# Second attention: the first pass's tiles issued whole and early in a step, and the output copy moved from VectorE to ScalarE

## The chip, the cores and the metric

The kernel runs on one core of a Trainium2 chip. The metric is device time in microseconds (us) for one execution. A core has a matrix engine (TensorE, in profiles PE, with its weight loads shown apart as PEld), a vector engine (VectorE, DVE), a scalar engine (ScalarE, ACT), GpSimd (POOL) and SyncE (SP), which issues the DMA transfers. Each engine works through its own instructions in order. They wait for each other through semaphores. Products of TensorE land in PSUM, from where DVE and ACT read them; POOL reads and writes SBUF alone.

## The reference

Two transformer layers follow one another on x of shape (4, 1024, 512), with 16 heads of 32 columns each. The first has a distance bias in its attention; the second has quantised linear layers and plain attention. The change touches only the second attention:

```
attn = softmax(einsum('bhqd,bhkd->bhqk', q, k) * hd ** (-0.5))   # per head: 1024 x 1024 scores
o    = einsum('bhqk,bhkd->bhqd', attn, v)                        # per head: 1024 x 32
```

There are 4 x 16 = 64 heads.

## The kernel before

The program is six stages with a barrier of all engines between them: the first layer's projections, attention and MLP, then the second's (`build_program`). `stage_attention1` is the second attention. q and k are held as high and low parts, so that one product over 96 rows (hi.hi, hi.lo, lo.hi) gives the scores at nearly full precision. Every head is computed in two passes:

- **First pass** (`score`, L707 to L714). A tile u has 128 queries as its partitions and 1024 keys as columns, in PSUM `s`, made by two products of 512 columns. DVE reduces each tile to the minimum of its rows (`minimum`, L799; q carries a factor of -1, so the minimum of a row is its softmax maximum). There are 8 tiles in a head, and `s` is a ring of 2 tiles: the first product of tile u+2 waits until DVE has reduced tile u. In tables of this document such a product is an `s` product.
- **Between the passes** POOL splits the 8 minima of each partition in two parts (`mm`), TensorE turns them to rows (`turn_minima`, L748), DVE copies these out (`mr`, L810), and SyncE puts them as rows 97 and 98 beside q.
- **Second pass** (`score_turned`, L716 to L723). The same scores again, turned: 128 keys as partitions and 512 queries as columns, with the minima taken in by the added rows. A tile is one product into PSUM `st`, a ring of 3 buffers of 512 columns. ACT takes the exponential of each into `PT` (`exponential`, L784). These are `st` products below. The rows that are turned, the minima's and the output's, take a buffer of the same ring.
- **Sums.** `times_v` multiplies `PT` by v into the left half of PSUM `po` (L733). POOL adds pairs of `PT` tiles into `two` (L866), and `total` multiplies those by ones into the right half of `po` (L741). `take_output` copies `po` to `ov` (L812 to L817), TensorE turns `ov` (`turn_output`, L754), and DVE divides (`output`, L819 to L831).

The work goes in steps w of 4 tiles (half a head), pipelined by hand: step w holds the first pass of tiles 4w to 4w+3, the second pass of tiles 4(w-4) and on, the products with v of step w-5, and in every second step a totals part or an output part. Steps in which the minima and the totals of a head stand are called even here, and those in which `ov` is copied and turned odd. A head takes one even and one odd step. There are 128 steps of first pass; in steps 4 to 127, 124 in number, both passes run side by side.

Nothing but the order in the code of each engine and the waits decides when something runs. Within a step the order on TensorE before is `st s st s` for each of the first three tiles and `st s s st` for the fourth: 8 `st` and 8 `s` products. The copy of `po` stands on DVE behind the first minimum of an odd step.

Of the kernel before, what the change touches and what calls it, by code (L numbers as in the profile page):

```python
# [6 lines left out]
ACT, ALU, AX = mybir.ActivationFunctionType, mybir.AluOpType, mybir.AxisListType  # L7

P = 128
B, L, D, H, F = 4, 1024, 512, 16, 2048  # L10
HD = D // H
T = B * L
DC, FC, LT = D // P, F // P, L // P
BLK = 512
# [382 lines left out]
N_HEADS = B * H  # L397
# [239 lines left out]
def stage_attention1(K):  # L637
# [4 lines left out]
    nc, a, pe, dve, act, pool, sp = K.nc, K.a, K.pe, K.dve, K.act, K.pool, K.sp  # L642
    ROWS = 3 * HD
    NW, TAIL = N_TILES // 4, 7
    with Stage(K, "T1") as S:
# [7 lines left out]
        ov = [S.sb(f"ov1{i}", [P, 2 * QW]) for i in range(2)]  # L653
        rec = [S.sb(f"rec1{i}", [P, 2, 4]) for i in range(2)]
        og = S.stores("og1", 2, [P, LT, GRP * HD])
        ps_r = S.ps_ring("s1", 2, [P, L])
        pst_r = S.ps_ring("st1", 3, [P, BLK])
        po = S.ps("po1", [P, 2 * QW])
        s_neg, s_score, s_min, s_mm, s_mt, s_mr, s_st, s_exp, s_two, s_pv, s_sum = (S.sem() for _ in range(11))
        s_row = [S.sem() for _ in range(2)]  # L660
        s_ov, s_turn, s_rec, s_out = (S.sem() for _ in range(4))
# [43 lines left out]
                store_group(g)  # L705
            og.done(sp)

        def score(u, g):
            n, t = divmod(u, LT)
            p, j = divmod(n, PAIR)  # L710
            qs, ks = qs_l.ready(pe, p), ks_l.ready(pe, p)
            ps = ps_r.take(pe, u, (s_min, u + 1)) if g == 0 else ps_r.at[u]
            nc.tensor.matmul(ps[:, g * BLK:(g + 1) * BLK], qs[0:ROWS, j, t * P:(t + 1) * P],  # L713
                             ks[0:ROWS, j, g * BLK:(g + 1) * BLK], start=True, stop=True).then_inc(*s_score.up())  # L714

        def score_turned(u, g):  # L716
            n, kb = divmod(u, LT)
            p, j = divmod(n, PAIR)
            pe.wait_ge(s_row[n % 2], 32 * (n // 2 + 1))
            pe.wait_ge(s_neg, 1)  # L720
            ps = pst_r.take(pe, ("st", u, g), (s_exp, 2 * u + g + 1))
            nc.tensor.matmul(ps[:], ks_l.at[p][0][0:ROWS + 2, j, kb * P:(kb + 1) * P], qs_l.at[p][0][0:ROWS + 2, j, g * BLK:(g + 1) * BLK],  # L722
                             start=True, stop=True).then_inc(*s_st.up())  # L723

        def times_v(u):
            n, kb = divmod(u, LT)
            p, j = divmod(n, PAIR)
            v = v_l.ready(pe, p)
            pe.wait_ge(s_exp, 2 * u + 2)
            if kb == 0:  # L730
                pe.wait_ge(s_ov, n)
            for g in range(4):
                op = nc.tensor.matmul(po[g * HD:(g + 1) * HD, 0:QW], v[:, kb, j * HD:(j + 1) * HD],  # L733
                                      pT[n % 2][:, kb, g * QW:(g + 1) * QW], start=kb == 0, stop=kb == LT - 1)
            op.then_inc(*s_pv.up())

        def total(m):
            n, k = divmod(m, LT // 2)
            pe.wait_ge(s_two, m + 1)
            for g in range(4):  # L740
                op = nc.tensor.matmul(po[g * HD:(g + 1) * HD, QW:2 * QW], K.ones[:, 0:HD], two[m % 6][:, g * QW:(g + 1) * QW],  # L741
                                      start=k == 0, stop=k == LT // 2 - 1)
            op.then_inc(*s_sum.up())

        def turn_minima(n):
            ps = pst_r.take(pe, ("min", n), (s_mr, n + 1))
            pe.wait_ge(s_mm, n + 1)
            nc.tensor.transpose(ps[0:2 * LT, 0:P], mm[n % 2][:].bitcast(F32).rearrange("p a t -> p (a t)"), K.ident[:]).then_inc(*s_mt.up())  # L748

        def turn_output(n):  # L750
            ps = pst_r.take(pe, ("out", n), (s_out, n + 1))
            pe.wait_ge(s_ov, n + 1)
            for i in range(2 * QW // P):
                op = nc.tensor.transpose(ps[:, i * P:(i + 1) * P], ov[n % 2][:, i * P:(i + 1) * P], K.ident[:])  # L754
            op.then_inc(*s_turn.up())

        def tensor_program():
            for w in range(NW + TAIL):
                for i in range(4):
                    if 0 <= w - 4 < NW:  # L760
                        score_turned(4 * (w - 4) + i, 0)
                    if w < NW:
                        score(4 * w + i, 0)
                    if w < NW and i == 3:
                        score(4 * w + i, 1)
                    if 0 <= w - 4 < NW:
                        score_turned(4 * (w - 4) + i, 1)
                    if w < NW and i < 3:
                        score(4 * w + i, 1)
                n, odd = divmod(w - 2, 2)  # L770
                if not odd and 0 <= n < N_HEADS:
                    turn_minima(n)
                n, odd = divmod(w - 7, 2)
                if not odd and 0 <= n < N_HEADS:
                    turn_output(n)
                if 0 <= w - 5 < NW:
                    for i in range(4):
                        times_v(4 * (w - 5) + i)
                n, odd = divmod(w - 6, 2)
                if not odd and 0 <= n < N_HEADS:  # L780
                    for i in range(LT // 2):
                        total(n * LT // 2 + i)

        def exponential(u, g):  # L784
            n, kb = divmod(u, LT)
            if n >= 2:
                act.wait_ge(s_pv, (n - 2) * LT + kb + 1)
                act.wait_ge(s_two, (n - 2) * LT // 2 + kb // 2 + 1)
            act.wait_ge(s_st, 2 * u + g + 1)
            nc.scalar.activation(pT[n % 2][:, kb, g * BLK:(g + 1) * BLK], pst_r.at["st", u, g][:], ACT.Exp, scale=-1.0).then_inc(*s_exp.up())  # L790

        def scalar_program():
            for w in range(NW + TAIL):
                if 0 <= w - 4 < NW:
                    for i in range(4):
                        exponential(4 * (w - 4) + i, 0)
                        exponential(4 * (w - 4) + i, 1)

        def minimum(u):  # L799
            n, t = divmod(u, LT)  # L800
            if t == 0 and n >= 2:
                dve.wait_ge(s_mm, n - 1)
            dve.wait_ge(s_score, 2 * (u + 1))
            nc.vector.tensor_reduce(mn[n % 2][:, t:t + 1], ps_r.at[u][:], AX.X, ALU.min).then_inc(*s_min.up())  # L804

        def take_minima(n):
            if n >= 2:
                dve.wait_ge(s_row[n % 2], 32 * (n // 2))
            dve.wait_ge(s_mt, n + 1)
            nc.vector.tensor_copy(mr[n % 2][:], pst_r.at["min", n][0:2 * LT, 0:P]).then_inc(*s_mr.up())  # L810

        def take_output(n):  # L812
            dve.wait_ge(s_pv, (n + 1) * LT)
            dve.wait_ge(s_sum, (n + 1) * LT // 2)
            if n >= 2:
                dve.wait_ge(s_turn, n - 1)
            nc.vector.tensor_copy(ov[n % 2][:], po[:]).then_inc(*s_ov.up())  # L817

        def output(n):  # L819
            h = n % H  # L820
# [15 lines left out]
        def vector_program():  # L836
            for w in range(NW + TAIL):
                if w < NW:
                    minimum(4 * w)
                n, odd = divmod(w - 7, 2)  # L840
                if not odd and 0 <= n < N_HEADS:
                    take_output(n)
                if w < NW:
                    for i in range(1, 4):
                        minimum(4 * w + i)
                n, odd = divmod(w - 2, 2)
                if not odd and 0 <= n < N_HEADS:
                    take_minima(n)
                n, odd = divmod(w - 7, 2)
                if not odd and 0 <= n < N_HEADS:  # L850
                    output(n)
# [28 lines left out]

        sync_program()
        tensor_program()
        vector_program()
        scalar_program()
        gpsimd_program()

# [1296 lines left out]
```

## Time and profile before

| | before |
|---|---|
| median of 3 runs (lowest to highest) | 3962.01 us (3960.73 to 3963.63) |
| the profiled execution: its own time | 3961.7 us |
| its span in the trace | 3959.9 us |
| second attention | from 2554 to about 3585 us of the span |
| busy over the whole span: PE, PEld, DVE, ACT, POOL | 93%, 62%, 63%, 58%, 42% |

Times in rows are microseconds from the start of the span, unless a column says ns. The duration of a matmul row is the time in the array with its pipeline, so two rows overlap; the distance between the starts of two products says how fast TensorE goes. A product that had to wait is shown from where it could start.

### The profile page before, as it was taken

The page shows a single profiled execution, that of the slowest core. Times are in us where ns is not written, and L with a number is a line of the kernel's source. Part 1 is how long each engine was busy: PE and PEld are TensorE (multiplying, and loading weights), DVE is VectorE, ACT ScalarE, POOL GpSimd, SP SyncE. Part 2 cuts the span into 40 slices and gives each one's busy share as a digit, 9 for nine tenths or more (in the row PEclk, how much of TensorE's full clock was granted, in tenths as well). Part 3 has the DMA queues.
Part 4 walks back from the last instruction along what each step waited for, and adds up shares of the span by engine and source line. Part 5 has one row for each costly group of instructions (what it writes and reads, how often), then busy time and mean ns, then how long its engine had stood idle before and what let it go on. Part 6 is the DMA issues. An engine that isn't in the chain of part 4 may idle for free. (4 is left out here: it accounts for less than half of the span.)

```text
span 3959.9 us, 68031 instructions
## 1 busy us (share of the span) xinstructions
PE 3671.7 (93%) x25924; PEld 2449.5 (62%) x25924; DVE 2510.9 (63%) x4095; ACT 2285.4 (58%) x3963; POOL 1672.8 (42%) x1931
## 2 busy tenths in 40 slices
PE   8997999999999987899999959799999999995999
PEld 7885666666666665778888845355555555552555
DVE  4335888888888867344431128676666666664987
ACT  2226888888888856222222218555555555554988
POOL 0004555555555557000000017466666666664554
PEclk9998999999999999999999979899999999997999
DMA  5445233333333179334431127823333333313221
GB/s 188 184 165 150 60 65 63 68 63 68 62 68 63 31 229 303 128 131 146 157 122 67 59 85 263 277 50 77 69 63 68 63 68 70 77 33 131 78 78 51
DMA packets 309604, 419.91 MB, mean 106 GB/s; under 512 B 90472, under 2 KB 167788, under 8 KB 309274
## 3 DMA queue, kind: packets, MB, share of 16 engines
q1 hardware_dynamic: 309280, 415.56, 37.4%
q8 instruction: 207, 3.39, 0.4%
q14 instruction: 117, 0.96, 0.1%
HBM read 257.34 MB, written 157.32 MB: 105 GB/s over the span
## 5 line engine op out<-in xcount | busy, mean ns | idle before, releaser
L790 ACT ACTIVATE PT<-st 128x512 f32<-128x512 f32 x1024 | 547.2, 604 | 482.4 <-PE st L722 473.6
L804 DVE TENSOR_REDUCE mn<-s 128x1 f32<-128x1024 f32 x512 | 598.6, 1219 | 336.8 <-PE s L713 236.5
L628 POOL TENSOR_SCALAR biastile<-dist,ascale 128x1024 f32<-128x1024 f32 x512 | 576.2, 1125 | 497.1 <-DVE mn L583 482.8
L866 POOL TENSOR_TENSOR two<-PT 128x1024 f32<-128x1024 f32 x256 | 608.6, 2378 | 364.9 <-ACT PT L790 364.8
L583 DVE CUSTOM_DVE_ANT_0 Sn<-sp,biastile 128x1024 f32<-128x1024 f32 x512 | 624.5, 1220 | 145.0 <-PE sp L489 113.5
L555 ACT ACTIVATE Sn<-Sn,mn 128x1024 f32<-128x1024 f32 x512 | 587.4, 1147 | 19.0 <-DVE mn L583 19.0
L521 PEld LDWEIGHTS pt<-ident,Sn 128*128 128x128 f32 x4096 | 440.5, 141 | 210.5 <-issue 206.7
L521 PE MATMUL pt<-ident,Sn 128*128 128x128 f32 x4096 | 561.6, 280 | 0.6 <-DVE PT L547 0.2
L713 PE MATMUL s<-KS,QS 96*128 96x512 f32 x1024 | 418.5, 432 | 79.1 <-DVE mn L804 46.5
L545 ACT ACTIVATE PT<-pt 128x512 f32<-128x512 f32 x640 | 369.4, 598 | 117.8 <-PE pt L521 117.8
L722 PE MATMUL st<-QS,KS 98*128 98x512 f32 x1024 | 421.6, 413 | 1.5 <-ACT PT L790 1.2
L1328 ACT ACTIVATE gf<-pf,b1T 128x512 f32<-128x512 f32 x128 | 88.3, 690 | 537.8 <-PE pf L1273 533.0
L489 PE MATMUL sp<-KS,QS 97*128 97x512 f32 x1024 | 366.8, 440 | 21.1 <-DMA KS<-cpad 18.7
L1734 POOL MEMSET rcD<- 128x128 bf16 x2 | 0.3, 206 | 775.0 <-POOLq L131 775.0
L510 PE MATMUL po<-PT,Vp 128*32 128x256 f32 x4096 | 325.7, 391 | 0.0
L1419 DVE TENSOR_TENSOR gl<-gf,gh 128x512 fp32r<-128x512 f32 x128 | 88.7, 693 | 372.8 <-ACT gh L1332 370.2
L713 PEld LDWEIGHTS s<-KS,QS 96*128 96x128 f32 x1024 | 186.7, 193 | 215.4 <-DVE mn L804 167.6
L547 DVE COPY PT<-pt 128x512 f32<-128x512 f32 x384 | 265.6, 692 | 59.4 <-PE pt L521 59.3
L722 PEld LDWEIGHTS st<-QS,KS 98*128 98x128 f32 x1024 | 194.4, 190 | 94.6 <-issue 51.9
L733 PE MATMUL po<-PT,Vp 128*32 128x256 f32 x4096 | 247.3, 382 | 0.0
L1284 PE MATMUL pacc<-w2h,gh 128*128 128x512 f32 x512 | 202.1, 395 | 0.6 <-DVE gl L1419 0.6
L1284 PE MATMUL pacc<-w2l,gh 128*128 128x512 f32 x512 | 202.3, 395 | 0.0
(257 smaller groups left out, 6099.8 us busy)
## 6 DMA issues: line engine op xcount, KB each, us to landing
QS<-s_qhi SPq DMA_DIRECT2D x128, 256.0 KB, 5.1
KS<-s_khi SPq DMA_DIRECT2D x128, 256.0 KB, 7.1
KS<-s_klo SPq DMA_DIRECT2D x64, 256.0 KB, 6.1
QS<-s_qlo SPq DMA_DIRECT2D x64, 256.0 KB, 6.9
Vp<-s_v SPq DMA_DIRECT2D x64, 256.0 KB, 7.7
s_o<-og SPq DMA_DIRECT2D x32, 512.0 KB, 4.1
xA<-in_x SPq DMA_DIRECT2D x8, 1024.0 KB, 5.8
s_qhi<-qstage SPq DMA_DIRECT2D x32, 256.0 KB, 2.0
```

What stands on the lines that cost most here:

```text
L489: op = nc.tensor.matmul(ps[:, g * BLK:(g + 1) * BLK], qs[0:rows_s, j, t * P:(t + 1) * P], ks[0:rows_s, j, g * BLK:(g + 1) * BLK], start=Tr ...
L521: op = nc.tensor.transpose(ps[:, i, :], sn[:, (g * HALF + i) * P:(g * HALF + i + 1) * P], K.ident[:])
L545: nc.scalar.activation(dst, src, ACT.Copy).then_inc(*s_cp_act.up())
L555: nc.scalar.activation(sn[:], sn[:], ACT.Exp, scale=-1.0, bias=mn[n % 3][:, t:t + 1], accum_out=sums[n % 5][:, t:t + 1]).then_inc(*s_exp.up())
L583: nc.vector.tensor_tensor_reduce(sn[:], sp_r.at[s][:], bt[s % 2][:], 1.0, 3.4e38, ALU.add, ALU.min, m).then_inc(*s_min.up())
L628: nc.gpsimd.tensor_scalar(bt[s % 2][:], dist[:, t, :], K.ascale[:, n % H:n % H + 1], 1.0, ALU.mult, ALU.mult).then_inc(*s_bias.up())
L713: nc.tensor.matmul(ps[:, g * BLK:(g + 1) * BLK], qs[0:ROWS, j, t * P:(t + 1) * P], ks[0:ROWS, j, g * BLK:(g + 1) * BLK], start=True, stop= ...
L722: nc.tensor.matmul(ps[:], ks_l.at[p][0][0:ROWS + 2, j, kb * P:(kb + 1) * P], qs_l.at[p][0][0:ROWS + 2, j, g * BLK:(g + 1) * BLK], start=Tr ...
L790: nc.scalar.activation(pT[n % 2][:, kb, g * BLK:(g + 1) * BLK], pst_r.at["st", u, g][:], ACT.Exp, scale=-1.0).then_inc(*s_exp.up())
L804: nc.vector.tensor_reduce(mn[n % 2][:, t:t + 1], ps_r.at[u][:], AX.X, ALU.min).then_inc(*s_min.up())
L866: nc.gpsimd.tensor_tensor(two[m % 6][:], pT[n % 2][:, 2 * k, :], pT[n % 2][:, 2 * k + 1, :], ALU.add).then_inc(*s_two.up())
L1284: op = nc.tensor.matmul(pacc[t][:], x[:, t * P:(t + 1) * P], w[:, f, :], start=f == 0 and n == 0, stop=f == FC - 1 and n == 2)
```

## The change

In TensorE's program the two products of a first-pass tile now stand together (`score(u)` without a half), and only the second of them raises the semaphore. A step's pattern is a list of pairs, (how many `st` products, then whether a whole `s` tile): `(1, 1), (1, 1), (3, 1), (2, 1), (1, 0)`. The copy of `po` to `ov` leaves DVE and is made by ACT with the function Copy, ahead of the exponentials of its step. DVE's four minima then stand in a row. The semaphores that the copy waits for and raises stay the same.

```diff
-        def score(u, g):
+        def score(u):
             n, t = divmod(u, LT)
             p, j = divmod(n, PAIR)
             qs, ks = qs_l.ready(pe, p), ks_l.ready(pe, p)
-            ps = ps_r.take(pe, u, (s_min, u + 1)) if g == 0 else ps_r.at[u]
-            nc.tensor.matmul(ps[:, g * BLK:(g + 1) * BLK], qs[0:ROWS, j, t * P:(t + 1) * P],
-                             ks[0:ROWS, j, g * BLK:(g + 1) * BLK], start=True, stop=True).then_inc(*s_score.up())
+            ps = ps_r.take(pe, u, (s_min, u + 1))
+            for g in range(L // BLK):
+                op = nc.tensor.matmul(ps[:, g * BLK:(g + 1) * BLK], qs[0:ROWS, j, t * P:(t + 1) * P],
+                                      ks[0:ROWS, j, g * BLK:(g + 1) * BLK], start=True, stop=True)
+            op.then_inc(*s_score.up())
 
         def tensor_program():
+            n_turned = n_first = 0
             for w in range(NW + TAIL):
-                for i in range(4):
+                for turned, first in ((1, 1), (1, 1), (3, 1), (2, 1), (1, 0)):
                     if 0 <= w - 4 < NW:
-                        score_turned(4 * (w - 4) + i, 0)
-                    if w < NW:
-                        score(4 * w + i, 0)
-                    if w < NW and i == 3:
-                        score(4 * w + i, 1)
-                    if 0 <= w - 4 < NW:
-                        score_turned(4 * (w - 4) + i, 1)
-                    if w < NW and i < 3:
-                        score(4 * w + i, 1)
+                        for _ in range(turned):
+                            score_turned(*divmod(8 * (w - 4) + n_turned, 2))
+                            n_turned = (n_turned + 1) % 8
+                    if w < NW and first:
+                        score(4 * w + n_first)
+                        n_first = (n_first + 1) % 4
 
+        def take_output(n):
+            act.wait_ge(s_pv, (n + 1) * LT)
+            act.wait_ge(s_sum, (n + 1) * LT // 2)
+            if n >= 2:
+                act.wait_ge(s_turn, n - 1)
+            nc.scalar.activation(ov[n % 2][:], po[:], ACT.Copy).then_inc(*s_ov.up())
+
         def scalar_program():
             for w in range(NW + TAIL):
+                n, odd = divmod(w - 7, 2)
+                if not odd and 0 <= n < N_HEADS:
+                    take_output(n)
                 if 0 <= w - 4 < NW:
...
-            dve.wait_ge(s_score, 2 * (u + 1))
+            dve.wait_ge(s_score, u + 1)
...
-        def take_output(n):
-            dve.wait_ge(s_pv, (n + 1) * LT)
-            dve.wait_ge(s_sum, (n + 1) * LT // 2)
-            if n >= 2:
-                dve.wait_ge(s_turn, n - 1)
-            nc.vector.tensor_copy(ov[n % 2][:], po[:]).then_inc(*s_ov.up())
...
                 if w < NW:
                     minimum(4 * w)
-                n, odd = divmod(w - 7, 2)
-                if not odd and 0 <= n < N_HEADS:
-                    take_output(n)
+                    minimum(4 * w + 1)
                 if w < NW:
-                    for i in range(1, 4):
-                        minimum(4 * w + i)
+                    minimum(4 * w + 2)
+                    minimum(4 * w + 3)
```

On TensorE, the first twelve products of an odd step before (`st` second pass, `s` first pass):

```order
L722 MATMUL st<-QS,KS 128x512
L713 MATMUL s<-KS,QS 128x512
L722 MATMUL st<-QS,KS 128x512
L713 MATMUL s<-KS,QS 128x512
L722 MATMUL st<-QS,KS 128x512
L713 MATMUL s<-KS,QS 128x512
L722 MATMUL st<-QS,KS 128x512
L713 MATMUL s<-KS,QS 128x512
L722 MATMUL st<-QS,KS 128x512
L713 MATMUL s<-KS,QS 128x512
L722 MATMUL st<-QS,KS 128x512
L713 MATMUL s<-KS,QS 128x512
```

And now, on TensorE, the whole of an odd step's 16 products and the four that turn `ov` (L714, L724 and L756 are the lines L713, L722 and L754 of before):

```order
L724 MATMUL st<-QS,KS 128x512
L714 MATMUL s<-KS,QS 128x512 x2
L724 MATMUL st<-QS,KS 128x512
L714 MATMUL s<-KS,QS 128x512 x2
L724 MATMUL st<-QS,KS 128x512 x3
L714 MATMUL s<-KS,QS 128x512 x2
L724 MATMUL st<-QS,KS 128x512 x2
L714 MATMUL s<-KS,QS 128x512 x2
L724 MATMUL st<-QS,KS 128x512
L756 MATMUL st<-ident,ov 128x128 x4
```

The first tile was complete with the fourth product and is now with the third; the second tile with the eighth and now the sixth. The third tile still begins with the tenth product, the fourth began with the fourteenth and now does too.

On DVE, an odd step and the even one behind it, before (`mn` minima, `ov` the output's copy, `rec` and `og` the division, `mr` the turned minima):

```order
L804 TENSOR_REDUCE mn<-s 128x1
L817 COPY ov<-po 128x512
L804 TENSOR_REDUCE mn<-s 128x1 x3
L827 RECIPROCAL rec<-st 128x8
L831 TENSOR_TENSOR og<-st,rec 128x4x32 x2
L804 TENSOR_REDUCE mn<-s 128x1 x4
L810 COPY mr<-st 16x128
```

And now the same two steps on DVE:

```order
L814 TENSOR_REDUCE mn<-s 128x1 x4
L830 RECIPROCAL rec<-st 128x8
L834 TENSOR_TENSOR og<-st,rec 128x4x32 x2
L814 TENSOR_REDUCE mn<-s 128x1 x4
L820 COPY mr<-st 16x128
```

The copy between the first and the second minimum is gone from here. On ACT it stands once in 16 exponentials now (an odd step and the even one behind it):

```order
L797 ACTIVATE ov<-po 128x512
L790 ACTIVATE PT<-st 128x512 x16
L797 ACTIVATE ov<-po 128x512
L790 ACTIVATE PT<-st 128x512 x16
```

Before, ACT had nothing but exponentials in this stage.

## Rows read from the trace of the kernel before

**Rows 1.** Stretches: us, busy and count per engine, granted clock, DMA share, GB/s
```profile
400.00:600.00 200.00, 200.00 (x1750) 126.11 (x1749) 167.30 (x301) 177.94 (x324) 108.04 (x96) 1.00 0.31 64
3100.00:3300.00 200.00, 188.78 (x1704) 115.16 (x1706) 135.17 (x165) 108.08 (x202) 125.00 (x76) 1.00 0.31 65
```
**Rows 2.** Waits from 2700 to 3500: total us, times, longest us
```profile
ACT PT L790 <- PE st L722: 360.4, 252, 3.6
...
DVE mn L804 <- PE s L713: 174.1, 51, 3.4
PEld s L713 <- DVE mn L804: 128.9, 202, 1.0
```
**Rows 3.** Timeline of PE, an odd step: start, us, engine, line, tiles
```profile
3009.68 0.50 PE L722 MATMUL st<-QS,KS 98*128 98x512 f32 x1
...
3010.50 0.40 PE L713 MATMUL s<-KS,QS 96*128 96x512 f32 x1
...
3011.67 0.40 PE L722 MATMUL st<-QS,KS 98*128 98x512 f32 x1
...
3012.21 0.50 PE L713 MATMUL s<-KS,QS 96*128 96x512 f32 x1
...
3013.02 0.40 PE L722 MATMUL st<-QS,KS 98*128 98x512 f32 x1
...
3013.94 0.73 PE L713 MATMUL s<-KS,QS 96*128 96x512 f32 x2 [0.53 <-DVE mn L804]
...
3014.51 0.40 PE L722 MATMUL st<-QS,KS 98*128 98x512 f32 x1
```
**Rows 4.** Timeline of PE, the even step ahead of it
```profile
3001.37 0.50 PE L722 MATMUL st<-QS,KS 98*128 98x512 f32 x1
...
3003.36 0.40 PE L722 MATMUL st<-QS,KS 98*128 98x512 f32 x1
...
3003.97 0.50 PE L713 MATMUL s<-KS,QS 96*128 96x512 f32 x1 [0.21 <-DVE mn L804]
...
3004.79 0.40 PE L722 MATMUL st<-QS,KS 98*128 98x512 f32 x1
...
3005.10 0.72 PE L713 MATMUL s<-KS,QS 96*128 96x512 f32 x2
3005.66 0.39 PE L722 MATMUL st<-QS,KS 98*128 98x512 f32 x1
...
3007.84 1.91 PE L741 MATMUL po<-two,ones 128*32 128x256 f32 x32
```
**Rows 5.** Timeline of DVE in the same two steps
```profile
3002.69 4.65 DVE L804 TENSOR_REDUCE mn<-s 128x1 f32<-128x1024 f32 x4 [1.68 <-POOL mm L859]
...
3010.93 1.23 DVE L804 TENSOR_REDUCE mn<-s 128x1 f32<-128x1024 f32 x1 [3.41 <-PE s L713]
...
3012.08 0.68 DVE L817 COPY ov<-po 128x512 f32<-128x512 f32 x1
...
3012.68 3.48 DVE L804 TENSOR_REDUCE mn<-s 128x1 f32<-128x1024 f32 x3
```
**Rows 6.** Timeline of ACT, the odd step; ACT and PE behind the last first-pass tile
```profile
3010.30 3.81 ACT L790 ACTIVATE PT<-st 128x512 f32<-128x512 f32 x7 [3.62 <-PE st L722]
...
3014.94 0.60 ACT L790 ACTIVATE PT<-st 128x512 f32<-128x512 f32 x1 [0.83 <-PE st L722]
...
3561.33 4.03 ACT L790 ACTIVATE PT<-st 128x512 f32<-128x512 f32 x8 [3.49 <-PE st L722]
...
3561.98 2.46 PE L722 MATMUL st<-QS,KS 98*128 98x512 f32 x5 [0.31 <-ACT PT L790]
```
**Rows 7.** Groups from 2700 to 3500: busy us, mean ns, idle before, releaser
```profile
L866 POOL TENSOR_TENSOR two<-PT 128x1024 f32<-128x1024 f32 x203 | 482.7, 2378 | 292.7 <-ACT PT L790 292.7
...
L817 DVE COPY ov<-po 128x512 f32<-128x512 f32 x50 | 34.0, 681 | 0.0
```
**Rows 8.** Groups of ACT from 400 to 1400, in the first attention
```profile
L545 ACT ACTIVATE PT<-pt 128x512 f32<-128x512 f32 x600 | 346.1, 597 | 112.0 <-PE pt L521 112.0
```

## The prediction

> **What bounds the stage.** I read four views in this order. First the stretches: in the middle of the second attention TensorE is busy 188.8 of 200 us at a granted clock of 1.00, DVE 135, POOL 125 and ACT 108 [rows 1]. TensorE is the engine to watch, but not all of its time is work. Then the waits: DVE and ACT wait for TensorE (174 and 360 us in 800), and these waits are the slack of engines that aren't the bound. TensorE in turn waits for something else: its weight load for an `s` product waits 128.9 us for a minimum of DVE, 202 times, which is four times in each of 50.7 heads [rows 2] (203 additions of POOL at four to a head give the same count, and 800 / 50.7 = 15.8 us for a head [rows 7]). Third, the timeline of one odd and one even step, to see which of these waits lengthen the step [rows 3, 4]. Fourth, DVE and ACT in the same steps [rows 5, 6].
>
> I count times in a step from its first `st` product. Without a stall the fourth product stands at 0.82 (3010.50 - 3009.68) and the ninth at 1.99 (3011.67): the first distance is 0.35 and every later one 0.235. So the 16th would stand at 0.35 + 14 x 0.235 = 3.64. It stands at 4.83 in the odd step (3014.51) and at 4.29 in the even one (3005.66 - 3001.37). The stalls cost 1.19 and 0.65 us, 1.84 us for a head.
>
> Each has one form. A product's weights load one slot ahead of it, so a product released late, at r, pays twice: it starts at r, and the next comes 0.35 and not 0.235 later. With L the start of the product ahead of it, its normal slot is L + 0.235, and the delay is r - L - 0.12. The four stalls by that: third tile odd 3012.21 - 3011.67 - 0.12 = 0.42, fourth tile odd 3013.94 - 3013.02 - 0.12 = 0.80, third tile even 3003.97 - 3003.36 - 0.12 = 0.49, fourth tile even 3005.10 - 3004.79 - 0.12 = 0.19 [rows 3, 4]. Their sum is 1.90, against 1.84 read from the starts; the form holds to a few hundredths.
>
> What releases them: in the odd step DVE's first minimum runs 3010.93 to 3012.16, and the third tile starts at 3012.21, 0.05 later. Then comes the copy, so the second minimum starts only at 3012.68, ends 3013.90, and the fourth tile starts at 3013.94 [rows 5]. The copy takes 0.60 of DVE's time there (3012.08 to 3012.68). The even step has no copy and a smaller second stall.
>
> **The change, part by part.**
> The paired tile. The first tile is complete with the third product, at 0.35 + 0.235 = 0.585, and its end is 0.40 behind that, at 0.985. Before it was the fourth (0.82, end 1.22). DVE began 0.03 after that end in the odd step (3010.93 against 3010.90) and 0.10 after in the even one (3002.69, step start 3001.37, so 1.32 against 1.22) [rows 3 to 5]. The first minimum now begins at 1.01 (odd) or 1.08 (even), 0.24 earlier, and frees its buffer at 1.01 + 1.22 + 0.05 = 2.28 or 2.35. The third tile's first product is still the tenth, L = 1.99: delay 0.17 or 0.24, in place of 0.42 and 0.49.
> The second minimum. DVE does a chain of four in 4.65, so 1.14 apart [rows 5]; the second tile is long complete. It frees its buffer at 3.42 (odd) or 3.49 (even). The fourth tile's first product is the fourteenth; the thirteenth then stands at L = 1.99 + 0.235 + 0.17 + 3 x 0.235 = 3.10, or 3.17. Delay 3.42 - 3.10 - 0.12 = 0.20 in both, in place of 0.80 and 0.19. Here the copy's 0.60 goes.
> Three `st` products in a row. `st` has three buffers. ACT starts the first exponential at 0.62 (3010.30), later ones 0.43 after their product (3014.94 against 3014.51), and no closer than 0.49 ((4.03 - 0.60) / 7 in the chain of eight), and a buffer is free 0.05 behind its end (3561.33 + 0.60, product at 3561.98) [rows 3, 6]. The eight `st` products now stand at 0, 0.82, 1.53, 1.76, 1.99, 2.86, 3.10 and 4.01; exponentials start at 0.62, 1.25, 1.96, 2.45, 2.94, 3.43. The seventh product needs the fourth exponential: 2.45 + 0.65 = 3.10, against L = 2.86, a delay of 0.12 by the form; but the fourth tile behind it waits for 3.42 anyway, which swallows it. The eighth needs the fifth, 3.59, and is at 4.01. The turned rows need the sixth, 4.08, against L = 4.01: nothing. No term.
> The copy on ACT. DVE needs 681 ns, ACT 597 for the same shape out of PSUM in the first attention [rows 7, 8]. It stands ahead of an odd step's exponentials and waits for the totals, whose last product ends at 3007.84 + 1.91 = 3009.75, 0.07 into the step [rows 4]. It starts at about 0.15, and at ACT's spacing of 0.49 the first exponential follows at 0.64 to 0.75 in place of 0.62. The second waits for its product until 1.25 either way. The cover is ACT's own wait for TensorE (360 us in 800, [rows 2]). Cost: zero. Its upper bound comes below as a rival. A gain can't come of it on ACT.
> What the copy meets: `po` is free earlier than at 3012.76, and the products with v that need it come after the 16th product. `ov` is needed for turning just there too. No term.
> One semaphore fewer per tile, the same number of products, loads and DMAs: no term. SyncE gets the turned minima as before, behind DVE's fourth minimum, at 1.08 + 4.65 = 5.7 into an even step, and the rows are wanted a step and a half later.
> POOL: four additions of 2.38 and two small operations make some 9.9 us in a head [rows 7], and a head will take 14.7.
>
> Here a rule speaks against the change. The rows say that ACT copies the shape in 0.60 us where DVE takes 0.68 [rows 7, 8]. The Trainium skill, "ScalarE: Activation LUTs", Rules for kernel authors, sends simple elementwise work to VectorE, which per element is up to about three times faster (it has bf16 in mind). By that, as an estimate, the copy would take ACT 3 x 0.68 = 2.04 us, the odd step would lose all it gains, and the time would stay near 3962. The trace prices the very shape and type, so the sum goes by it.
>
> **The sum.** The odd step's 16th product moves from 4.83 to 3.64 + 0.37 = 4.01, 0.82 earlier. The even step's moves from 4.29 to 3.64 + 0.44 = 4.08, 0.21 earlier. What follows the 16th product (turned rows, products with v, totals) waits for nothing that the change delays. 1.03 us for a head, in 124 / 2 = 62 heads' worth of steps in which both passes run: 64 us. In the four first steps only `s` products run, in the last only `st` ones, in the order of before. The other stages are untouched. From the profiled execution's own 3961.7 that gives 3898; the runs' median is 3962.0, 0.3 above, within their spread of 2.9.
>
> **Bounds.** If no stall were left at all, 1.84 x 62 = 114 us go: 3848. If half of the left-over 0.81 us goes too, 3873. On the other side, if ACT doesn't overlap two exponentials when three products come close together, they stand 0.60 apart: 1.96, 2.56, 3.16, 3.76, 4.36. The seventh product is then at 3.21, which the fourth tile's wait nearly swallows, but the turned rows (which need the sixth exponential's buffer) are released at 3.76 + 0.65 = 4.41 against L = 4.01, and pay 4.41 - 4.01 - 0.12 = 0.28 in every step. The gain falls to (1.03 - 0.56) x 62 = 29 us: 3933. The row nearest to the case is the chain of eight at 0.49, so I take that.
>
> **Rivals.**
> (A) The `st` ring becomes the bound, as just worked out: 3933. For it: three `st` products stand together, and ACT has the copy too. Against it: the chain of eight at 0.49 with the same ring [rows 6].
> (B) The stalls stay and only move: DVE starts its minimum earlier but the `s` products stall just as long, because what counts is DVE's spacing; then only the copy's 0.60 in the odd step goes, 0.60 x 62 = 37 us: 3925. Against it: the first minimum starts on the end of a tile, both before and now, and DVE has been idle for 3.41 us there [rows 5].
> (C) Slower: the copy blocks ACT. If it starts at d into the odd step, the first exponential starts at d + 0.49 and its buffer is free at d + 1.14, the next at d + 1.63; the fourth and fifth `st` products wait for these, and from the fifth on the rest takes some 1.8 us, so the 16th product stands at about d + 3.4. Before it was at 4.83. With the even step's 0.21 won, the head is slower from d = 1.6 on. At d = 2 the odd step loses 0.6, a head 0.4, and the time is 3962 + 24 = 3986. For it: ACT was free of any wait on `po`, and everything of the step is queued behind the copy. Against it: the totals end 0.07 into the step, and DVE started within 0.03 to 0.10 of the product it waited for.
> (D) The clock: TensorE's denser work brings a lower granted clock. It would take about 0.93 in the stage to eat 64 us. Against it: in the first attention TensorE is busy 200.00 of 200 us at 1.00 [rows 1]. If the clock fell by half of that, 3930.
> (E) The change does nothing to the time, because TensorE waits elsewhere: 3962. Against it: DVE and ACT both wait for TensorE.
>
> **Numbers.** 3898 has a chance of 0.74, with its own range 3880 to 3912; A and B together 0.13, D's mild form 0.03, C 0.04, E 0.03, and more gained than 3880 says 0.03. Range for 8 in 10: 3878 to 3925. Two executions of this kernel can be told apart from about 0.2%, 8 us. Faster by more: 0.93; within: 0.03; slower: 0.04.
>
> **What would show it.** In the changed kernel's timeline: a head every 14.7 us; the 16th product 4.0 to 4.1 into a step, and both steps alike; the first minimum at 1.0 to 1.1; third tile at 2.3, fourth at 3.4 to 3.5; DVE's four minima in one chain of 4.65 in both steps; the copy on ACT at about 0.15 with 0.60, and the second exponential at 1.25. The wait of `s` weight loads for DVE falls from 0.64 us each to some 0.3. I'd be wrong if the seventh `st` product or the turned rows wait for ACT (A), if the tenth product is as late as before (B), or if the first exponential of an odd step is later than about 1.1 (C).

## The result, and the profile after

| | before | changed |
|---|---|---|
| median | 3962.82 us of 4 (3960.73 to 3964.3) | 3899.4 us of 4 (3897.8 to 3901.37) |
| ratio to before, 95% interval | | 0.9841 (0.9824 to 0.9858) |
| profiled execution, its own time and span | 3961.7, 3959.9 us | 3899.86, 3898.0 us |
| last division of the second attention starts at | 3585.64 us | 3521.60 us |

The kernel is 63 us faster; the interval makes that 56 to 70 us. The forecast was 3898 with a range of 3878 to 3925.

The stretch view, in the middle of the second attention (us, busy and count of PE, PEld, DVE, ACT, POOL, granted clock, DMA share, GB/s), answers to [rows 1]:

```profile
3100.00:3300.00 200.00, 200.00 (x1791) 123.24 (x1789) 137.66 (x166) 124.33 (x234) 132.86 (x83) 1.00 0.36 74
```

TensorE now shows 200.00 us busy in 200, at the same clock. That looks like the end of all waiting. It isn't: a matmul row of 0.40 us overlaps the next, 0.235 behind it, and such an overlap hides a stall of up to 0.16 us. The weight-load column, 123 of 200 us, still has room. The waits of 2700 to 3500, which answer to [rows 2], show what is left:

```profile
DVE mn L814 <- PE s L714: 249.6, 107, 3.2
ACT ov L797 <- PE po L743: 171.9, 54, 3.2
...
PEld st L724 <- ACT PT L790: 48.4, 224, 0.8
PEld s L714 <- DVE mn L814: 46.5, 214, 0.3
```

The weight loads of `s` products wait 46.5 us in place of 128.9, 0.22 each in place of 0.64. And a row is new: the `st` loads wait 48.4 us for ACT's exponentials, 224 times. DVE and ACT now each hold a weight load of TensorE for a short time, four times in a head.

The timeline of PE in one even step (from 3002.31) and one odd step (from 3010.41), against [rows 3, 4]. An x2 row is two products. The second starts 0.235 behind the first, or 0.34 where the first was held:

```profile
3002.31 0.50 PE L724 MATMUL st<-QS,KS 98*128 98x512 f32 x1
...
3004.67 0.73 PE L714 MATMUL s<-KS,QS 96*128 96x512 f32 x2
3005.24 0.64 PE L724 MATMUL st<-QS,KS 98*128 98x512 f32 x2
3005.80 0.73 PE L714 MATMUL s<-KS,QS 96*128 96x512 f32 x2
3006.37 0.40 PE L724 MATMUL st<-QS,KS 98*128 98x512 f32 x1
...
3010.41 0.50 PE L724 MATMUL st<-QS,KS 98*128 98x512 f32 x1
...
3012.69 0.73 PE L714 MATMUL s<-KS,QS 96*128 96x512 f32 x2
3013.25 0.73 PE L724 MATMUL st<-QS,KS 98*128 98x512 f32 x2
3013.82 0.73 PE L714 MATMUL s<-KS,QS 96*128 96x512 f32 x2
3014.39 0.40 PE L724 MATMUL st<-QS,KS 98*128 98x512 f32 x1
```

DVE and ACT in the same steps, against [rows 5, 6]:

```profile
3003.39 4.62 DVE L814 TENSOR_REDUCE mn<-s 128x1 f32<-128x1024 f32 x4 [1.43 <-PE s L714]
...
3010.59 0.60 ACT L797 ACTIVATE ov<-po 128x512 f32<-128x512 f32 x1 [3.18 <-PE po L743]
...
3011.09 4.33 ACT L790 ACTIVATE PT<-st 128x512 f32<-128x512 f32 x8
...
3011.41 4.61 DVE L814 TENSOR_REDUCE mn<-s 128x1 f32<-128x1024 f32 x4 [3.22 <-PE s L714]
```

Read against the start of their steps:

| from the first product of the step | before | forecast | changed |
|---|---|---|---|
| first minimum, odd / even | 1.25 / 1.32 | 1.01 / 1.08 | 1.00 / 1.08 |
| third tile, odd / even | 2.53 / 2.60 | 2.28 / 2.35 | 2.28 / 2.36 |
| fourth tile, odd / even | 4.26 / 3.73 | 3.42 / 3.49 | 3.41 / 3.49 |
| 16th product, odd / even | 4.83 / 4.29 | 4.01 / 4.08 | 3.98 / 4.06 |
| copy on ACT, first exponential, odd | - / 0.62 | 0.15 / 0.64 to 0.75 | 0.18 / 0.68 |

### The profile page after: what moved, and what is told of

Its sections match the earlier page's. It is cut to its first block and busy times, and to the rows that moved or that the text cites. A ratio compares the mean times of both kernels' runs of the same rounds, so it can differ in the third digit from the quotient of the medians.

```text
span 3898.0 us, 67727 instructions
## 1 busy us (share of the span) xinstructions
PE 3656.5 (94%) x25868; PEld 2448.2 (63%) x25924; DVE 2469.4 (63%) x4031; ACT 2316.0 (59%) x4027; POOL 1663.2 (43%) x1931
## 5 line engine op out<-in xcount | busy, mean ns | idle before, releaser
L714 PE MATMUL s<-KS,QS 96*128 96x512 f32 x1024 | 356.8, 431 | 25.0 <-DMA KS<-s_khi 23.6
L724 PE MATMUL st<-QS,KS 98*128 98x512 f32 x1024 | 369.5, 421 | 1.3 <-ACT PT L790 1.3
L724 PEld LDWEIGHTS st<-QS,KS 98*128 98x128 f32 x1024 | 192.8, 189 | 139.0 <-ACT PT L790 59.4
L714 PEld LDWEIGHTS s<-KS,QS 96*128 96x128 f32 x1024 | 177.1, 194 | 106.1 <-DVE mn L814 64.3
```

The costliest lines, as they stand in the source:

```text
L714: op = nc.tensor.matmul(ps[:, g * BLK:(g + 1) * BLK], qs[0:ROWS, j, t * P:(t + 1) * P], ks[0:ROWS, j, g * BLK:(g + 1) * BLK], start=True, ...
```

## The experiments

All changes are to `stage_attention1`. The median of before in these sessions was 3962.6 to 3964.9 us. In the code, `...` marks lines left out, and what stands behind `#` is not in the kernels.

**The copy on ACT alone.** TensorE's order stays as before. Against the kernel before, only `take_output` moves, from DVE's program to ACT's:

```diff
+        def take_output(n):
...
+            nc.scalar.activation(ov[n % 2][:], po[:], ACT.Copy).then_inc(*s_ov.up())
+
         def scalar_program():
             for w in range(NW + TAIL):
+                n, odd = divmod(w - 7, 2)
+                if not odd and 0 <= n < N_HEADS:
+                    take_output(n)
...
-            nc.vector.tensor_copy(ov[n % 2][:], po[:]).then_inc(*s_ov.up())
```

> The order on TensorE as before, only the output's copy moved to ACT. My theory (the stalls are r - L - 0.12 behind DVE's minima): in the odd step the second minimum ends at 1.25 + 1.14 + 1.22 = 3.61, the fourth tile is released at 3.66 against L = 3.34, a delay of 0.20 in place of 0.80: 0.60 x 62 = 37 us gained, 3925. The even step stays at 4.29 for its 16th product. Rival (the copy gains nothing by itself, the early tile does all): 3962. Rival (the copy on ACT delays the first exponentials): above 3962.

Measured: 3926.9 us, ratio 0.9914 (0.9898 to 0.9931), where 3925 was expected. In its timeline the odd step, which starts at 3008.33, has one chain of four minima and the fourth tile 3.66 behind the start, where it was 4.26:

```profile
3009.58 4.64 DVE L814 TENSOR_REDUCE mn<-s 128x1 f32<-128x1024 f32 x4 [3.42 <-PE s L713]
...
3010.86 0.50 PE L713 MATMUL s<-KS,QS 96*128 96x512 f32 x1
...
3011.99 0.72 PE L713 MATMUL s<-KS,QS 96*128 96x512 f32 x2
```

The third tile has not moved (3010.86 - 3008.33 = 2.53). So this half of the change works on the fourth tile of odd steps alone, and is worth 0.60 us a head.

**The order alone.** The changed kernel with `take_output` back on DVE, behind the first minimum:

```diff
                 if w < NW:
                     minimum(4 * w)
+                n, odd = divmod(w - 7, 2)
+                if not odd and 0 <= n < N_HEADS:
+                    take_output(n)                 # on DVE; gone from ACT
+                if w < NW:
                     minimum(4 * w + 1)
```

> TensorE's new order, the copy on DVE behind the first minimum as before. Theory: the first minimum is 0.24 earlier, the third tile's delay falls to 0.17 (odd) and 0.24 (even); the fourth tile in the odd step still waits for copy plus second minimum, 3.42 + 0.60 = 4.02 against L = 3.10, 0.80. Odd 16th product at 3.64 + 0.97 = 4.61 (before 4.83), even at 4.08 (before 4.29): 0.43 x 62 = 27 us, 3935. Rival (the order does all, the copy's engine nothing): 3898. Rival (only the copy counts, stalls just move): 3962.

Measured: 3935.2 us, ratio 0.9932 (0.9917 to 0.9947), where 3935 was expected. An odd step there starts at 3013.25. DVE and PE:

```profile
3014.26 1.23 DVE L804 TENSOR_REDUCE mn<-s 128x1 f32<-128x1024 f32 x1 [3.22 <-PE s L714]
...
3015.40 0.68 DVE L817 COPY ov<-po 128x512 f32<-128x512 f32 x1
...
3015.54 0.73 PE L714 MATMUL s<-KS,QS 96*128 96x512 f32 x2
...
3017.27 0.73 PE L714 MATMUL s<-KS,QS 96*128 96x512 f32 x2 [0.39 <-DVE mn L804]
```

The third tile is at 2.29, as in the changed kernel; the fourth is at 4.02 and still waits for the copy and the second minimum. The two parts alone gain 36 and 27 us against the before of their own session (3962.6), which adds up to the 63 that both gain together.

**The copy on DVE, one minimum later.** Is it the engine, or the place in its queue?

```diff
                 if w < NW:
                     minimum(4 * w)
                     minimum(4 * w + 1)
+                n, odd = divmod(w - 7, 2)
+                if not odd and 0 <= n < N_HEADS:
+                    take_output(n)                 # on DVE; gone from ACT
```

> The new order, the copy on DVE, but behind the second minimum of the odd step and not the first. Theory (what counts is what stands ahead of the second minimum, not the engine of the copy): both tiles are released as in the changed kernel, the third minimum is 0.60 later and nobody waits for it within the step, ov is ready at about 4.0, when its turning is due: 3899 to 3905. Rival (taking work from DVE is what counts, since it has 0.68 us more per head): 0.60 x 62 = 37 us slower than the changed kernel, 3936.

Measured: 3897.8 us, ratio 0.9837 (0.9822 to 0.9851), the same as the changed kernel. The odd step starts at 3007.64; the second minimum ends at 3011.00, the fourth tile's products begin at 3011.11, 3.47 in, and the last `st` product is at 3.97, where the changed kernel has it at 3.98:

```profile
3008.64 2.36 DVE L804 TENSOR_REDUCE mn<-s 128x1 f32<-128x1024 f32 x2 [3.21 <-PE s L714]
...
3010.91 0.68 DVE L817 COPY ov<-po 128x512 f32<-128x512 f32 x1
...
3011.11 0.67 PE L714 MATMUL s<-KS,QS 96*128 96x512 f32 x2
...
3011.61 0.40 PE L724 MATMUL st<-QS,KS 98*128 98x512 f32 x1
```

The tile's weights load at 3.41 (3011.05), as in the changed kernel. Its product starts 0.06 later because the seventh `st` product ahead of it came late: ACT released that one's load only at 3010.77, 3.13 in. DVE does as much work as before the change and the gain is whole. Moving the copy to ACT was one way of getting it from between the first and the second minimum; nothing came of DVE's lighter load.

**Half a minimum.** It takes one of the two left-over holds away:

```diff
-            nc.vector.tensor_reduce(mn[n % 2][:, t:t + 1], ps_r.at[u][:], AX.X, ALU.min)
+            nc.vector.tensor_reduce(mn[n % 2][:, t:t + 1], ps_r.at[u][:, 0:BLK], AX.X, ALU.min)
```

> The changed kernel, but the minimum is taken over the first 512 of the 1024 keys only, which leaves the second half out. A minimum should take some 0.69 us and not 1.22, so both s stalls go. Theory (the ring of st with ACT's exponentials stands right behind DVE as the next wait): the seventh st product is released at 3.10 against L = 2.70, 0.28 late, the 16th product stands at 3.92 in both steps in place of 3.98 and 4.06: 0.2 x 62 = 13 us, about 3887. Rival (DVE's minima are all that is left): both 16th products at 3.64, 0.76 x 62 = 47 us, 3852.

Measured: 3879.9 us, ratio 0.9792 (0.9777 to 0.9806), where 3887 was expected and the rival had 3852. A minimum takes 0.69 us in place of 1.22 and DVE's busy time falls from 138 to 89 us in 200, but the gain over the changed kernel is 19.5 us and not 47. The waits from 2700 to 3400 name the next one:

```profile
DVE mn L814 <- PE s L714: 389.7, 292, 4.0
...
PEld st L724 <- ACT PT L790: 63.3, 291, 0.3
```

There is no row for `s` waiting on DVE any more, and in the odd step that starts at 2999.70 the 16th product stands at 3003.57, 3.87 in, not at the unheld 3.64. The expectation had said 3.92 for both steps; the even one is at 3.88, and these 0.05 and 0.04 are 6 of the 7 us between 3887 and 3879.9. The ring of `st` stands close behind DVE.

**The copy three times.** How deep is the cover on ACT?

```diff
+        scr = [S.sb(f"scr1{i}", [P, 2 * QW]) for i in range(2)]
...
+            act.settle()
+            for buf in scr:                        # two buffers nobody reads
+                nc.scalar.activation(buf[:], po[:], ACT.Copy).then_inc(*act.own.up())
             nc.scalar.activation(ov[n % 2][:], po[:], ACT.Copy).then_inc(*s_ov.up())
```

> The changed kernel, with the output's copy made three times on ACT (twice more, into two buffers nobody reads, ahead of the real one). Theory (ACT's wait for its first products is a cover of only about half a microsecond, and beyond it the ring of st passes the delay to TensorE): the copies start at 0.18, the first exponential at 0.18 + 3 x 0.49 = 1.65 in place of 0.68, the fourth st product is released at 2.30 and the 16th product stands at 1.16 + 3.4 = 4.6 in the odd step in place of 3.98: 0.6 x 62 = 37 us slower than the changed kernel, 3937. The even step stays at 4.06. Rival (ACT has 40% idle time, so one more us of it in 15 costs nothing): 3900. Rival (all 0.98 us go onto the step): 3899 + 61 = 3960.

Measured: 3938.1 us, ratio 0.9937 (0.9923 to 0.9951), where 3937 was expected. The odd step that starts at 3014.42:

```profile
3014.61 1.09 ACT L800 ACTIVATE scr<-po 128x512 f32<-128x512 f32 x2 [3.18 <-PE po L744]
...
3016.06 2.58 ACT L791 ACTIVATE PT<-st 128x512 f32<-128x512 f32 x5
```

and on TensorE:

```profile
3016.73 0.99 PE L725 MATMUL st<-QS,KS 98*128 98x512 f32 x2 [0.40 <-ACT PT L791]
...
3019.00 0.40 PE L725 MATMUL st<-QS,KS 98*128 98x512 f32 x1
```

The first exponential is at 1.64, the fourth `st` product at 2.31 (the first of the two rows), the 16th product at 4.58 (the second). One copy costs nothing; 0.98 us more ahead of the exponentials costs 0.60 of each odd step. Rival C's arithmetic (d + 3.4, with the last copy at d = 1.16, makes 4.56) holds; only its condition wasn't met by one copy.

**Two products and not three ahead of the third tile.**

```diff
-                for turned, first in ((1, 1), (1, 1), (3, 1), (2, 1), (1, 0)):
+                for turned, first in ((1, 1), (1, 1), (2, 1), (2, 1), (2, 0)):
```

> The changed kernel with the pattern (1, 1), (1, 1), (2, 1), (2, 1), (2, 0): two st products and not three ahead of the third tile. Theory: the third tile's first product is the ninth, so L = 1.76 against a release at 2.28 or 2.35, held 0.40 or 0.47 in place of 0.17 or 0.24; then the fourth tile is released at 3.42 or 3.49 against L = 3.10 or 3.17. The 16th product stands at 4.24 or 4.31 in place of 3.98 or 4.06: 0.26 + 0.25 for a head, 31 us slower than the changed kernel, 3931. Rival (pairing is what counts, not where the third tile stands): 3899.

Measured: 3936.5 us, ratio 0.9931 (0.9917 to 0.9945), 37 us slower than the changed kernel, where 31 was expected. In the step that starts at 3011.21 the third tile is released at the same 2.29 (3013.50), but it is the ninth product, so TensorE stands idle for longer ahead of it. The 16th product stands at 4.22 in this step (4.24 expected) and at 4.30 in the even one (4.31 expected). What the forecast lacks comes behind it, at the end of the odd step:

```profile
3015.19 0.64 PE L724 MATMUL st<-QS,KS 98*128 98x512 f32 x2
...
3015.70 0.42 PEld L756 LDWEIGHTS st<-ident,ov 128*128 128x128 f32 x4 [0.30 <-ACT PT L790]
```

The turned output waits for the sixth exponential's buffer. From the 16th product to the first product with v it takes 0.85 us, 0.77 in the changed kernel, which is 5 us in 62 heads. The forecast had left that out here, though the prediction had followed it for its own pattern.

**The fourth tile last.** By the two chains there is a better order:

```diff
-                for turned, first in ((1, 1), (1, 1), (3, 1), (2, 1), (1, 0)):
+                for turned, first in ((1, 1), (2, 1), (2, 1), (3, 1)):
```

> The changed kernel with the pattern (1, 1), (2, 1), (2, 1), (3, 1): the third st product stands ahead of the second tile, and the fourth tile is last. Theory (both chains, DVE's minima and ACT's exponentials, have to be fed as early as they can take it): the second tile is still complete before the first minimum ends; the third exponential starts at 1.74 and not 1.96, so the seventh product is no longer held, the eighth is released at 3.37 against L = 3.10, 0.15 late, and the fourth tile behind it comes unheld. The 16th product stands at 3.95 in both steps, 0.03 and 0.11 earlier than now: 0.14 x 62 = 9 us, about 3890. Rival (only DVE's two releases at 2.28 and 3.42 matter, and the tile that is last waits for neither): 16th product at 3.64 + 0.17, 0.17 and 0.18 earlier, 22 us, 3877. Rival (nothing to be had): 3899.

Measured: 3888.3 us, ratio 0.9812 (0.9799 to 0.9826), where 3890 was expected. In the odd step from 3004.61 the fourth tile starts at 3008.30, 3.69 in (0.23 for its second product makes 3.92 for the 16th), and its rows name no wait:

```profile
3006.90 0.73 PE L714 MATMUL s<-KS,QS 96*128 96x512 f32 x2
3007.47 1.00 PE L724 MATMUL st<-QS,KS 98*128 98x512 f32 x3
3008.30 0.63 PE L714 MATMUL s<-KS,QS 96*128 96x512 f32 x2
```

What held TensorE there is the eighth `st` product, by its weight load at 3.36, where 3.37 was expected:

```profile
3007.97 0.19 PEld L724 LDWEIGHTS st<-QS,KS 98*128 98x128 f32 x1 [0.30 <-ACT PT L790]
```

By the two ratios to before the kernel is 11 us faster than the changed one. Their intervals hardly overlap (0.9799 to 0.9826 against 0.9824 to 0.9858).

**A wait moved.** The table of starts has the first minimum 0.08 later in even steps than in odd ones. In the kernel before it began 0.10 behind its tile's end in even steps and 0.03 in odd ones. In even steps it waits for two semaphores, its tile's and POOL's `mm`; the edit gives the second wait to a DVE instruction of the step before:

```diff
                 if not odd and 0 <= n < N_HEADS:
+                    dve.wait_ge(s_mm, min((w + 1) // 2, N_HEADS) - 1)
                     output(n)
```

> The changed kernel, with the wait of an even step's first minimum for POOL's split of the minima moved half a head earlier, to the division of the step before (POOL is two steps past it). One look: in an even step the first minimum starts 0.10 us behind the end of its tile, in an odd one 0.03. Theory (an instruction that waits for two semaphores starts some 0.07 later): the even step's first minimum starts at 1.00 and not 1.08, the third tile at 2.29 and not 2.36, and the time is 0.07 x 62 = 4 us less, too little to tell by time. Rival (the 0.07 is of the even step's own, as POOL's work or the minima's buffer): it stays at 1.08.

In the even step that starts at 3001.13 the minimum is at 1.01 and the third tile at 2.29:

```profile
3002.14 4.62 DVE L814 TENSOR_REDUCE mn<-s 128x1 f32<-128x1024 f32 x4 [1.37 <-PE s L714]
...
3003.42 0.73 PE L714 MATMUL s<-KS,QS 96*128 96x512 f32 x2
```

The single run, 3896.5 us, can't tell 4 us, but the starts can. The profile named `mm` as the releaser of this minimum in [rows 5]. It can't have been: in the changed kernel POOL's `mm` of the step ends at 3003.96, and the minimum has begun at 3003.39. The wait is for the `mm` of a head earlier, raised long before.

**Both.** The late order with the wait moved:

> order_late and early_wait together. Theory: with the new pattern the eighth st product is held by the fifth exponential until 3.37 in both steps, which is behind what DVE's first minimum holds; so the even step's earlier minimum (1.01, third tile at 2.29) moves the third tile, but the eighth st product and all behind it stay: fourth tile at 3.69 or 3.70 in both steps, 3888. Rival (each 0.07 of a held tile comes off the step): 3884, the fourth tile at 3.63 in the even step.

Measured: 3887.6 us, ratio 0.9806 (0.9793 to 0.982), 3888 expected. The even step from 3001.25 has its first minimum at 1.01 and the third tile at 3003.53, 2.28; the fourth tile stays at 3.69 (3004.94), as the ring of `st` lets it:

```profile
3003.53 0.73 PE L714 MATMUL s<-KS,QS 96*128 96x512 f32 x2
3004.10 1.00 PE L724 MATMUL st<-QS,KS 98*128 98x512 f32 x3
3004.94 0.63 PE L714 MATMUL s<-KS,QS 96*128 96x512 f32 x2
```

The times alone (3887.6 against a rival's 3884) wouldn't have told the theories apart; the start of the fourth tile does.

## Why the prediction was right

**What bounds the stage.** TensorE, with 1.84 us of stalls in a head, all behind DVE's minima: confirmed from both sides. What brings a release forward moves the time by its whole amount (the two parts alone), and putting the copy back on DVE, one place later, costs nothing.

**The form r - L - 0.12.** It gave the 16th product within 0.05 us wherever a variant's was forecast, and within 0.03 and 0.02 in the changed kernel. By it a release 0.24 earlier is worth 0.24, and a load that is 0.12 late costs nothing.

**The paired tile** was to be worth 0.25 in the third tile of both steps, of which the even step gives a little back: 0.21 forecast for the whole even step, 0.23 measured. **The copy's place** was to be worth 0.60 in the odd step: 36 us by itself, 37 forecast.

**The `st` ring** (no term) costs nothing, as forecast, but it is closer than the prediction's list says. The loads wait for ACT, 0.22 each, and it is two different products. The load of the fifth `st` product waits for the second exponential until 1.88 (odd) and 1.89 (even) into the step, which the prediction didn't list for its pattern; against L = 1.76 that is the 0.12 that cost nothing. The seventh waits for the fourth exponential, as listed, in the odd step until 3.07. By the form the next slot is then 0.35 behind that, 3.42, level with DVE's release of the fourth tile at 3.41: the held tile swallows the wait with nothing to spare. These are the two loads of the odd step:

```profile
3012.29 0.19 PEld L724 LDWEIGHTS st<-QS,KS 98*128 98x128 f32 x1 [0.19 <-ACT PT L790]
...
3013.48 0.19 PEld L724 LDWEIGHTS st<-QS,KS 98*128 98x128 f32 x1 [0.27 <-ACT PT L790]
```

That the ring could become the bound was seen in the bounds (rival A, 3933), and the half minimum measured it. A's condition, exponentials no closer than 0.60, failed: eight of them would take 8 x 0.60 = 4.80 us and take 4.33 in the odd step, waits for their products included.

**The copy on ACT** cost nothing: the first exponential went from 0.62 to 0.68, and the buffer of the second comes free at the same time in the odd step, with the copy, as in the even one, without it (1.88 and 1.89). The row of 597 ns for the shape in the first attention was right to a nanosecond:

```profile
L797 ACT ACTIVATE ov<-po 128x512 f32<-128x512 f32 x55 | 32.8, 597 | 176.6 <-PE po L743 171.9 <-issue 4.7
```

The Trainium skill, "ScalarE: Activation LUTs", Rules for kernel authors, sends relu, max, min, add and mul to VectorE, up to about 3 times faster in bf16. Applied to this copy, fp32 out of PSUM, it would point the wrong way: 597 ns on ACT against 681 on DVE [rows 7]. But neither does it matter which of them does it, as the copy on DVE one place later shows.

**The sum.** 64 us were forecast, and the end of the stage came 3585.64 - 3521.60 = 64.0 earlier. That it agrees to the last digit is luck. A head went from 15.77 to 14.71 us, 1.06 where 1.03 was forecast; the 61 heads from step 6 on give 64.8, and the six steps ahead of them and a start of the stage 0.3 earlier give 0.8 together. The first step that has `st` products alone then takes 9.12 us in place of 7.51 and gives 1.6 back. In it the products with v take 3.50 us (before 1.93), and the granted clock is 0.54, close to the lower of TensorE's two levels, 1.2 GHz. Before, it was 1.00 there. The two rows, before and changed:

```profile
3557.12 1.93 PE L733 MATMUL po<-PT,Vp 128*32 128x256 f32 x32
...
3491.53 3.50 PE L735 MATMUL po<-PT,Vp 128*32 128x256 f32 x32
```

The stretches of the changed kernel's step, in the columns of [rows 1]:

```profile
3487.50:3491.20 3.70, 3.42 (x12) 1.42 (x8) 0.00 (x0) 3.04 (x7) 2.54 (x4) 1.00 0.00 0
3491.20:3494.90 3.70, 3.70 (x38) 1.71 (x41) 0.28 (x1) 0.99 (x3) 3.70 (x2) 0.54 0.15 44
```

In both kernels the `st` products just ahead of this wait for ACT. The step takes 9.12 us in the run with the copy on DVE one place later too, and 7.49 in the one with the copy on ACT alone; why the clock falls in some runs and not in others stays open. So rival D, the clock, fails in the long part of the stage (1.00 from 2700 to 3487) and shows up once behind it. Rival B fails by the third tile, which moved 0.25 and 0.24 earlier.

The span is shorter by 61.9 only: from that last division to the end it takes 376.4 us in place of 374.3. That stage is not touched by the change. 1.7 of the 2.1 us lie between its first two reductions on DVE, the second of which waits for the DMA into `oF` (3592.39 to 3599.37 before, 3528.28 to 3536.97 changed).

## What to carry to other kernels

On an engine that waits in order, price a change by the two products beside each wait: when the one ahead started, when the awaited buffer comes free. The order within a step can then be worked out to some hundredths of a microsecond. What matters of a neighbour's work is what it does between the wait's source and the next one, not its load: a copy moved by one place was worth as much as a copy moved to another engine. Feed each of two consumers as early as it can take it, and put last what is released last.

## What was not expected of the hardware

- TensorE's busy time read 200.00 of 200 us while 0.76 us of each head, 5%, were still stalls (3.98 and 4.06 against an unheld 3.64). Half the minimum gained 19.5 us from that "full" engine. Starts show it, durations don't.
- The first minimum of a step, where it waits for two semaphores, started 0.10 us behind its tile's end, and where it waits for one, 0.03. With the second wait moved to an earlier instruction the start came 0.07 earlier, though that semaphore had been raised about a head before. Two traces show it.
